# First search of a layer kernel: 16-bit masks counted by TensorE, fewer columns on ScalarE, turned modulation products, GpSimd splits in quarters

## What is computed

```
adj = emb_s * emb_t * softmax(x, -1) / sqrt(512); diagonal = -inf
x   = x + (1 at the 5120 largest of adj, else 0)
ada = cond @ ada_w + ada_b        # 4 x 3072: shift, scale, gate, twice
x1  = ln(x) * (1 + scale1) + shift1
q, k, v = x1 @ qkv_w + qkv_b;  16 heads of 128
x   = x' + gate1 * (softmax(q k') v @ out_w + out_b)
x   = x + gate2 * (gelu(ln(x)*(1+scale2)+shift2 @ w1 + b1) @ w2 + b2), all added to x'
```

## Time and profile before

| | us |
|---|---|
| median of 3 runs | 1551.48 (1547.79 to 1551.97) |
| the profiled execution: its own time | 1549.28 |
| its span | 1547.5 |
| PE busy | 1499.1 (97%) |
| DVE busy | 1107.3 (72%) |
| ACT busy | 884.3 (57%) |
| POOL busy | 424.2 (27%) |

### The profile page before, as it was taken

One profiled execution on the slowest core, in us unless ns is written; L12 is line 12 of the kernel. 1 busy time (PEld: TensorE's weight loads), 2 busy tenths in 40 slices (PEclk: granted clock), 3 DMA queues, 4 the chain that ended last, 5 costly groups with the idle time before them and its releaser, 6 DMA issues.

```text
span 1547.5 us, 22147 instructions
## 1 busy us (share of the span) xinstructions
PE 1499.1 (97%) x7157; PEld 1244.7 (80%) x7157; DVE 1107.3 (72%) x2572; ACT 884.3 (57%) x1631; POOL 424.2 (27%) x371
## 2 busy tenths in 40 slices
PE   1999999999999999999999999999999999999998
PEld 1878788879788888888878887888878888888987
DVE  7878887777796887876784887876786666664431
ACT  4656777765846566662753666663572655554340
POOL 6714555554021422331000432232000232223000
PEclk9999999999999999999999999999999999999999
DMA  7866899996767677775465788686465686776463
GB/s 293 300 265 191 230 225 267 255 250 241 257 247 246 172 198 202 207 188 182 172 225 217 196 208 197 155 215 206 164 232 190 191 218 160 196 214 158 182 238 118
DMA packets 338611, 327.65 MB, mean 212 GB/s; under 512 B 274848, under 2 KB 279104, under 8 KB 335424
## 3 DMA queue, kind: packets, MB, share of 16 engines
q1 hardware_dynamic: 338208, 325.91, 71.0%
q10 hardware_dynamic: 288, 0.33, 0.1%
HBM read 204.54 MB, written 54.54 MB: 167 GB/s over the span
## 4 chain that ended last, share of the span: by engine, by line
PE 90%; DVE 4%; DVEq 1%; DMA 1%; ACT 1%; issue 1%; SPq 1%; POOL 0%; ACTq 0%; POOLq 0%
PE bank L1395 27%; PE bank L1397 27%; PE bank L1396 27%; PE bank L1717 2%; PE bank L1615 1%; PE bank L1610 1%; PE bank L1611 1%; DVE tb L1027 1%; PE bank L1427 1%; DVEq L1218 1%; DMA w<-split_weights 1%; SPq L537 1%; PE bank L1449 1%; PE bank L1446 1%; PE bank L1445 1%
## 5 line engine op out<-in xcount | busy, mean ns | idle before, releaser
L740 POOL CAST probT<-turned 128x1024 fp32r<-128x1024 f16 x256 | 260.1, 1053 | 679.5 <-PE bank L1397 355.0
L1395 PE MATMUL bank<-xT,w 128*128 128x512 f32 x704 | 279.7, 397 | 0.0
L1396 PE MATMUL bank<-xT,w 128*128 128x512 f32 x704 | 273.9, 389 | 0.0
L1397 PE MATMUL bank<-xT,w 128*128 128x512 f32 x704 | 273.8, 389 | 0.0
L883 ACT ACTIVATE prob<-bank,nbias 128x512 f32<-128x512 f32 x256 | 176.2, 689 | 107.9 <-DVE nbias L1219 98.8
L1236 DVE SCALAR_TENSOR_TENSOR halves<-prob,rinv,halves 128x512 f16<-128x512 f32 x256 | 176.0, 750 | 27.2 <-ACT halves L890 27.2
L890 ACT ACTIVATE halves<-prob,rinv 128x512 f16<-128x512 f32 x256 | 163.8, 712 | 30.6 <-DVE rinv L1232 23.9
L1217 DVE TENSOR_REDUCE rowmax<-bank 128x1 f32<-128x512 f32 x256 | 174.4, 681 | 0.0
L1397 PEld LDWEIGHTS bank<-xT,w 128*128 128x128 f32 x704 | 132.2, 188 | 28.0
L1395 PEld LDWEIGHTS bank<-xT,w 128*128 128x128 f32 x704 | 132.9, 189 | 25.0
L1396 PEld LDWEIGHTS bank<-xT,w 128*128 128x128 f32 x704 | 132.4, 188 | 24.9
(11 more groups left out here) (171 smaller groups left out, 3314.7 us busy)
## 6 DMA issues: line engine op xcount, KB each, us to landing
w<-split_weights SPq DMA_DIRECT2D x154, 1024.0 KB, 5.6
split_weights<-w SPq DMA_DIRECT2D x38, 1024.0 KB, 6.8
wraw<-weights_in SPq DMA_DIRECT2D x48, 512.0 KB, 4.8
split_weights<-xT SPq DMA_DIRECT2D x7, 1024.0 KB, 8.0
adaw<-ada_w_in SPq DMA_DIRECT2D x4, 1536.0 KB, 13.0
xr<-x_in SPq DMA_DIRECT2D x4, 1024.0 KB, 5.7
turned<-halves SPq DMA_TRANSPOSE x256, 3.3
split_weights<-qk SPq DMA_DIRECT2D x3, 1024.0 KB, 7.6
```

The costliest lines, as they stand in the source:

```text
L740: nc.gpsimd.tensor_copy(probT[:, :, :, i * P:(i + 1) * P].rearrange("p a j t -> p (a j) t"), turned_of(h)[:, i, :, :]).then_inc(widened, 1)
L1395: pe.matmul(dst, w_hi_ap, x_hi_ap, start=first, stop=False)
L1396: pe.matmul(dst, w_hi_ap, x_lo_ap, start=False, stop=False)
L1397: return pe.matmul(dst, w_lo_ap, x_hi_ap, start=False, stop=last)
```

## The change

In the search of sequence 0 alone:
1. **Masks.** DVE gets 1408 columns. Their 16-bit keys are copied by ACT into a dense tile `first16` before the search (three copies, each behind one part of the keys). In each step DVE writes a 0/1 mask in float16 in two pieces, 768 and 640 columns. PE adds the mask up with eleven one-column products (mask block as weights, ones as moving column) into bank 5, DVE copies that column to `cnt_v`, and the two products of before follow. For the second level DVE rebuilds `first16` from `low`: a clamp of 128x1408 floats and a conversion to 16 bits.
2. **ScalarE** counts 640 columns.
3. **Modulation.** `cond`'s four columns are the weights and `ada_w` moves: six products of 512 columns before step 0, thirty of 256 columns behind steps 2 to 31, six behind the search. The result has four partitions: ACT copies it out of six banks, PE turns it with 24 small transposes, and ACT copies `ada` from bank 5. The first part of `ada_w` is loaded ahead of the raw halves, each part with a semaphore of its own.
4. **GpSimd.** The scaling and the splits run in pieces of 256 columns, with a drain between a half's casts and its subtractions. (`split_pieces` serves the 14 splits ahead of the block alone.)

```diff
-FIRST_V, FIRST_S = 992, 1056
+FIRST_V, FIRST_S = 1408, 640
+PIECE = 256
+CHUNKS = ((0, 768), (768, FIRST_V))
...
-ADA_STEP = 8
+ADA_STEP = 2
+ADA_BANKS = (0, 1, 2, 4, 6, 7)
...
             sp.wait_ge(x0_in[NT - 1], 16)
+            sp.dma_start(adaw[:, 0, :], ada_w[0:P, :]).then_inc(ada_in[0], 16)
             load_raw(0, 2)
-            for c in range(C):
-                sp.dma_start(adaw[:, c, :], ada_w[c * P:(c + 1) * P, :]).then_inc(ada_in, 16)
+            for c in range(1, C):
+                sp.dma_start(adaw[:, c, :], ada_w[c * P:(c + 1) * P, :]).then_inc(ada_in[c], 16)
...
+            def split_pieces(k, hi, lo):
+
+                for at in range(0, HALF, PIECE):
+                    part = slice(at, at + PIECE)
+                    ins = nc.gpsimd.tensor_copy(hi[:, part], wraw[:, k % 2, part])
+                ins.then_inc(w_hi, 1)
+                pool.drain()
+                for at in range(0, HALF, PIECE):
+                    part = slice(at, at + PIECE)
+                    ins = nc.gpsimd.tensor_tensor(lo[:, part], wraw[:, k % 2, part], hi[:, part].bitcast(F32),
+                                                  ALU.subtract)
+                ins.then_inc(w_ready, 1)
...
-                nc.gpsimd.tensor_scalar(low[:, :], keys16[:, :, 0], UNIT, None, ALU.mult).then_inc(low_scaled, 1)
+                for at in range(0, 2 * NCOUNT, PIECE):
+                    ins = nc.gpsimd.tensor_scalar(low[:, at:at + PIECE], keys16[:, at:at + PIECE, 0], UNIT, None, ALU.mult)
+                ins.then_inc(low_scaled, 1)
...
             topk_exp(0)
+            for i in range((FIRST_V + T - 1) // T):
+                act_e.wait_ge(keyed, i + 1)
+                part = slice(i * T, min((i + 1) * T, FIRST_V))
+                nc.scalar.copy(first16[:, part], keys16[:, part, 1]).then_inc(first_filled, 1)
...
             act_e.wait_ge(ada_done, 1)
-            nc.scalar.copy(ada[:, :, :].rearrange("p m b -> p (m b)"), bank[0][:, 0:6 * C * B]).then_inc(ada_raw, 1)
+            for part in range(6):
+                nc.scalar.copy(ada_row[0:B, part * D:(part + 1) * D], bank[ADA_BANKS[part]][0:B, :])\
+                    .then_inc(ada_copied, 1)
+            act_e.wait_ge(ada_turned, 1)
+            nc.scalar.copy(ada[:, :, :].rearrange("p m b -> p (m b)"), bank[5][:, 0:6 * C * B]).then_inc(ada_raw, 1)
...
+            def count_by_masks(step):
+
+                for lo, hi in CHUNKS:
+                    V.tensor_scalar(masks[:, lo:hi], first16[:, lo:hi], cand[:, :], None, op0=ALU.is_ge)\
+                        .then_inc(masked, 1)
+                far = TOP_BIT / (1 << step % LEVEL) / 2
+                V.tensor_scalar(bounds[:, 0:1], cand[:, :], -far, None, ALU.add)
+                V.tensor_scalar(bounds[:, 1:2], cand[:, :], far, None, ALU.add)
+                dve.drain()
+                dve.wait_ge(col_summed, step + 1)
+                with nc.allow_low_precision(reason=EXACT):
+                    V.tensor_copy(cnt_v[:, :], bank[5][:, 0:1]).then_inc(counted_v, 1)
...
+                if is_t0(t) and step == STEPS - 1:
+                    V.tensor_scalar(cand[:, :], cand[:, :], UNIT, None, ALU.mult).then_inc(cand_ready, 1)
+                    dve.drain()
...
+                    if is_t0(t):
+                        V.tensor_scalar(clamped[:, :], low[:, :FIRST_V], 0.0, UNIT * (2 * TOP_BIT - 1), ALU.max, ALU.min)
+                        dve.drain()
+                        V.tensor_scalar(first16[:, :], clamped[:, :], 1.0 / UNIT, None, ALU.mult)
+                        dve.drain()
...
             topk_keys(0, 0, NT)
+            dve.wait_ge(first_filled, (FIRST_V + T - 1) // T)
             start_level(0, 0)
...
+                    for n, (lo, hi) in enumerate(CHUNKS):
+                        pe.wait_ge(masked, len(CHUNKS) * step + n + 1)
+                        for at in range(lo, hi, P):
+                            ins = pe.matmul(bank[5][:, 0:1], masks[:, at:at + P], ones[:, 0:1],
+                                            start=at == 0, stop=at + P == FIRST_V)
+                    ins.then_inc(col_summed, 1)
...
+            def ada_part(c, part, cols):
+
+                if cols.start == 0 and part == 0:
+                    pe.wait_ge(ada_in[c], 16)
+                return pe.matmul(bank[ADA_BANKS[part]][0:B, cols], small[:, c0 + c * B:c0 + (c + 1) * B],
+                                 adaw[:, c, part * D + cols.start:part * D + cols.stop], start=c == 0, stop=c == C - 1,
+                                 skip_group_check=True)
+
+            pe.wait_ge(small_in, 16)
+            for part in range(6):
+                ada_part(0, part, slice(0, D))
+            pieces = [(c, part, half) for c in range(1, C) for part in range(6) for half in (slice(0, 256), slice(256, D))]
...
+                if step >= ADA_STEP:
+                    ada_part(*pieces[step - ADA_STEP])
+            for piece in pieces[STEPS - ADA_STEP:]:
+                ins = ada_part(*piece)
             ins.then_inc(ada_done, 1)
             take_ranks(0)
+            pe.wait_ge(ada_copied, 6)
+            for m in range(6 * C):
+                ins = pe.transpose(bank[5][:, m * B:(m + 1) * B], ada_row[0:B, m * P:(m + 1) * P], ident[0:B, 0:B])
+            ins.then_inc(ada_turned, 1)
             pe.wait_ge(w_ready, 1)
```

More of the change, by code:

```diff
@@ L204, in count_split, with unit @@
     return FIRST_V if is_t0(t) else NCOUNT
-def unit(step):
-    return UNIT if step >= LEVEL else 1.0
+def unit(t, step):
+    return UNIT if step >= LEVEL and not is_t0(t) else 1.0
 def first_splits(h):
@@ L340, in block_kernel, with total @@
         bank = [ctx.enter_context(nc.psum_tensor(f"bank{i}", [P, 512], F32)) for i in range(8)]
-        def total(step):
-            return bank[6 if step < HEAD_STEPS else 3]
+        def total(t, step):
+            return bank[6 if step < HEAD_STEPS and not is_t0(t) else 3]
         def sem(name):
             return ctx.enter_context(nc.semaphore(name))
-        small_in, ada_in, xn_in, tb_in = sem("small_in"), sem("ada_in"), sem("xn_in"), sem("tb_in")
+        small_in, xn_in, tb_in = sem("small_in"), sem("xn_in"), sem("tb_in")
+        ada_in = [sem(f"ada_in{c}") for c in range(C)]
+        keyed, first_filled, masked, col_summed = (sem("keyed"), sem("first_filled"), sem("masked"),
+                                                   sem("col_summed"))
+        ada_copied, ada_turned = sem("ada_copied"), sem("ada_turned")
         xr_in = sem("xr_in")
@@ L777, in topk_count @@
                 with nc.allow_low_precision(reason=EXACT):
-                    nc.scalar.activation(passed_s[:, :2 * NCOUNT - at], src, ACT.Sign, bias=cand[:, :], scale=-1.0,
+                    nc.scalar.activation(passed_s[:, :2 * NCOUNT - at], src, ACT.Sign, bias=cand[:, :],
+                                         scale=-1.0 / UNIT if is_t0(t) and step >= LEVEL else -1.0,
                                          accum_out=cnt_s[:, :]).then_inc(counted_s, 1)
@@ L786, in topk_sides @@
                                          accum_out=sign_sum[:, :]).then_inc(signs_summed, 1)
[L787 removed]
+                nc.scalar.mul(far_cand[:, :], cand[:, :], -FAR / UNIT).then_inc(far_ready, 1)
                 act_e.wait_ge(far_ready, t * 2 + 1)
                 act_e.wait_ge(ties_counted, t + 1)
[L790 removed]
+                nc.scalar.activation(low[:, :], low[:, :], ACT.Identity, bias=far_cand[:, :], scale=FAR / UNIT)\
                     .then_inc(far_ready, 1)
@@ L1022, in count @@
             def count(t, step):
-                end = count_split(t)
-                src = keys16[:, :end, 1] if step < LEVEL else low[:, :end]
+                if is_t0(t):
+                    count_by_masks(step)
+                    return
+                src = keys16[:, :NCOUNT, 1] if step < LEVEL else low[:, :NCOUNT]
                 with nc.allow_low_precision(reason=EXACT):
-                    V.tensor_scalar(passed_v[:, :end], src, cand[:, :], None, op0=ALU.is_ge, op1=ALU.add,
+                    V.tensor_scalar(passed_v[:, :NCOUNT], src, cand[:, :], None, op0=ALU.is_ge, op1=ALU.add,
                                     accum_out=cnt_v[:, :]).then_inc(counted_v, 1)
[L1029 to L1033, removed]
+            def count_by_masks(step):
[9 more added lines that the diff above has]
+                    V.tensor_copy(cnt_v[:, :], bank[5][:, 0:1]).then_inc(counted_v, 1)
             def start_level(t, step):
-                V.memset(cand[:, :], (TOP_BIT - 0.5) * unit(step)).then_inc(cand_ready, 1)
+                V.memset(cand[:, :], (TOP_BIT - 0.5) * unit(t, step)).then_inc(cand_ready, 1)
                 dve.drain()
```

48 lines of the change are left out of this document (22 added, 26 removed).

## The result

The median of four runs after the change is 1571.6 us (1569.5 to 1572.8), against 1549.6 us for the kernel before in the same comparison (1547.7 to 1552.0): a ratio of 1.014, with a 95% interval of 1.0118 to 1.0161. The change makes the kernel slower by about 22 us. The profiled execution took 1571.56 us with a span of 1569.5, 22.0 more than before's.

A forecast was written before the change was run, and what follows sets the result against it. One chain releases every engine at the block, so the work ahead of it, mainly DVE's search steps, decides. Terms +1.0 - 2.6 + 16 + 2.4 + 0.2 + 6.5 = +23.5 on 1549.3 gave 1573 us, range 1549 to 1589.

The forecast's parts named there:

- Steps without POOL: Search steps with POOL idle: 1.88 us each, 0.08 less than now, -2.6 us over thirty-two steps.
- POOL's waits: Search steps: masks wait for POOL's pieces on the shared port, 0.6 us a step over 27 steps, +16 us.
- the second mask: In each search step, a waiting POOL piece gets in between the two masks, costing 0.4 us.
- The alternation of 1.9 and 2.8: Search in the changed profile: steps were to alternate between 1.9 and 2.8 us, and be 1.9 with POOL idle.
- The start: Ahead of the search: six modulation products delay the first move to 21.0 from 20.00, +1.0 us (0.6 to 4.2).
- Between the levels: Between the search's two levels: clamp, conversion and one wait for a POOL piece, +2.4 us (1.9 to 3.5).
- the end: At the end of the search: the last scaling of cand, +0.2 us.
- Behind the search: After the search: ACT's copies, 24 transposes and 40 unread products delay z's transposes by +6.5 us (+4 to +7.7).
- Ahead of the block everything is on the path: Before the block, at about 100 us: one chain releases every engine, so a later start moves the end equally.
- What waits for POOL is needed 10 us later: Behind the search: the desks' saves and the gates, which wait for POOL, are needed 10 us or more later.
- With POOL's waits gone: Search steps: no waits for POOL at all give +7.5, 1557 us; within the little-waiting rival, chance 0.16.
- ScalarE never decided: Search steps: rival that ScalarE's count decides, steps of 1.57 us, result -5.4, 1544 us; chance 0.16.

The follow-up runs named there:

- the thinned: The changed kernel with POOL's casts and subtractions in the 14 splits on 16 columns of each 256, tiles cleared first: 1562.5 us, 1.0086.
- the whole POOL: The changed kernel with POOL's scaling, casts and subtractions in pieces of 1024 columns instead of 256: 1586.4 us, 1.0243.
- the eight kernels without a warm-up: Kernels with turned modulation products but without 130 unread PE products ahead of the first six; those six took 6.87 to 8.22 us.
- the kernel of 1548.6: The kernel before with turned modulation products and new load order, 8 and 18 unread products around the transposes: 1548.6 us, 0.9994.
- the quarters alone: The kernel before with only POOL's scaling and splits in pieces of 256 columns: 1556.8 us, 1.0046.
- three parts mended: The changed kernel with one mask a step, 8 and 18 unread products, and 130 unread products ahead of the first six: 1566.2 us, 1.0106.
- the mended one with halves: The changed kernel with one mask, 8 and 18 unread products, 130 early unread products, and POOL pieces of 512 columns: 1562.8 us, 1.0089.

## Why the prediction was right

The forecast of 1573 us was right in time, sign and mechanism. That it came within 2 us is luck in part: the start and the steps without POOL came out 4.0 us dearer than forecast, and POOL's waits 3.9 us cheaper.

- **Steps without POOL**, -2.6 forecast: too good. The step was put at 1.88 and is 1.95 with POOL almost idle, against 1.968 before: -0.5 over 30 intervals. The masks cost 0.71 together, not 0.59. The step's claim that the round trip eats the masks' gain is shown, and so fully that nothing is left.
- **POOL's waits**, +16 forecast: the mechanism is shown by the thinned and the whole POOL, and the size is 30 x (2.353 - 1.95) = 12.1 us, 0.40 a step instead of 0.6 over 27 steps. The mis-sized term is the second mask: a piece doesn't get into every gap. One mask in place of two takes away 0.21 a step, which is what the gap was worth, where 0.4 was put on it. The alternation of 1.9 and 2.8 was not seen in the first level, where steps were 2.25 and 2.41 in turn. POOL ended at T - 0.9, not at T - 4.
- **The start**, +1.0 forecast and 0.6 to 4.2 as bounds: +2.9. The load landed at 13.89 and not near 13.1, the six products took 8.13 and not 7.2, and from their end to the first move it took 0.88, not 0.7. The 7.2 let these products stand at the lower clock level as long as the unread ones of the earlier trace rows did; the eight kernels without a warm-up took 6.87 to 8.22, so it fits some of them, and the profiled execution was one of the slowest.
- **Between the levels**, +2.4: +2.1; **the end**, +0.2: +0.2.
- **Behind the search**, +6.5: +6.2, with PE's row as foretold (ACT's copies, transposes, 40 products, no idle time). Rearranging the row alone takes it back: to T + 15.86 in the changed kernel, to T + 15.50 with the modulation alone.
- **Ahead of the block everything is on the path**: in the change, within what the runs can tell (22.95 us at `z`, 22.0 at the end). In the kernel of 1548.6 it was not: 2.15 us at `z` left at most 0.5.
- **What waits for POOL is needed 10 us later**: true in the changed kernel, and only there. It was the cover for the quarters, and the prediction didn't price its loss. With the quarters alone that is 6 to 7 us. Nor did it price what a wait of PE does to the clock level behind it.
- **Rivals.** With POOL's waits gone 1557 was given for the kernel; the thinned one, less the 3.4 us of its clearing, is at 1559. ScalarE never decided: in every step it waited for the candidate, for 1.0 us at least.
- **The sums.** Added up again, the parts of a step give 1.89 and not 1.88, those behind the search +6.4 and not +6.5, and 40 products at the later rate of the earlier trace rows take 8.4 us and not 8.8. None of it changes the forecast.

None of these kernels beats the one before. The best, the turned modulation with fewer unread products, is level with it.

## What to carry to other kernels

A faster operation on a serial route pays only by what it takes off the whole round: 0.5 us saved on DVE went into one more pass through PE and back, so write out the new round in full before counting the gain. If the new operation is of a kind that waits for GpSimd, as these masks were, GpSimd's instructions beside it come on the path, and each gap between two such operations is a place where a piece gets in. Here one long mask was better than two short ones, and shorter GpSimd pieces helped only until their fixed parts made GpSimd itself late. When a mend removes one wait, look up what was late behind it, and what TensorE's clock level is after it; gains that were measured one at a time didn't add up. And read a term in the profiles of several kernels that share the code before calling a microsecond of it won.

## What the runs showed of the hardware

DVE's two-input operations hold GpSimd up as hard as GpSimd holds up the masks: four 256-column casts of together 1.04 us' worth of data took 8.46 us across a scan, a combination and an addition, one piece begun in each gap and one beside the next operation, while these grew only from 4.42, 2.35 and 1.23 us to 4.78, 2.48 and 1.26.

The granted clock of the search differs between the kernels. Windows of the changed kernel inside its two levels:

```profile
22.00:58.00 36.00, 26.09 (x252) 11.33 (x252) 25.24 (x91) 13.86 (x30) 34.62 (x60) 0.56 0.59 200
63.00:100.00 37.00, 27.89 (x255) 11.77 (x255) 26.42 (x95) 14.66 (x32) 31.83 (x56) 0.50 0.75 264
```

The column behind the five engines (PEclk) reads 0.56 and 0.50, the lower level (1.2 GHz) in most or all of the stretch, where before read 1.00. Yet the 40 unread products take the same in both, 11.18 and 11.13, and in both they begin at half rate. Two windows of the changed kernel's, of these products alone:

```profile
111.00:115.00 4.00, 3.71 (x9) 2.93 (x10) 0.50 1.03 420
117.00:121.00 4.00, 4.00 (x20) 3.29 (x19) 1.00 0.80 310
```

Here the clock shown goes with the rate, 0.50 and then 1.00; in the kernel before 10 and then 19 products stood under a shown 1.00. So a shown 1.00 ahead of the block didn't mean that PE was at its upper level; the durations of products of a known size are the surer reading. The shown drop goes with the turned modulation and not with the masks. The row of the page for the turned modulation alone, with the old count, then for the quarters alone:

```profile
PEclk8579999999999999999999999999999999999999
```
```profile
PEclk9989999999999999999999999999999999999999
```

In the first the mean interval is 1.969 us and in the kernel before 1.968. That doesn't price the lower level for a step, since by the reading above the search before may have run at it too.

A wait of PE shows in the clock behind it: after 4.37 us (quarters alone) and 3.70 us (three parts mended) of idle time the block began with products of 0.63 to 0.77 us, after 0.50 us (changed kernel, and the mended one with halves) with 0.39 to 0.47 us.
